# The last expert mixture of a four-layer kernel: the turn of a token tile is issued two beats ahead of its product, and VectorE writes the tiles' row numbers

## What is computed

```python
xn = _layernorm(x, ln_gamma, ln_beta)
xf = xn.reshape(-1, D)                                  # 2048 tokens, D = 128
probs = softmax(clip(xf @ router_w.T))                  # 8 experts
topk_p, topk_i = jax.lax.top_k(probs, 2)
for eid in range(8):
    xe = xf * dense_gate[:, eid:eid + 1]
    gate, up = jnp.split(xe @ gate_up_w[eid].T, 2, axis=-1)   # 256 each
    out = out + (jax.nn.silu(gate) * up) @ down_w[eid].T
return x + out.reshape(B, S, D)                         # and a layer norm behind it
```

## Time and profile before

| | us |
|---|---|
| median of three runs | 1167.92 (1166.6 to 1170.28) |
| the profiled execution, its own time | 1160.82 |
| its span in the trace | 1159.1 |
| from the first turn of the stage (1037.4) to the span's end | 121.7 |

### The profile page before, as it was taken

One profiled execution on the slowest core, in us unless ns is written; L12 is line 12 of the kernel. 1 busy time (PEld: TensorE's weight loads), 2 busy tenths in 40 slices (PEclk: granted clock), 3 DMA queues, 4 the chain that ended last, 5 costly groups with the idle time before them and its releaser, 6 DMA issues.

```text
span 1159.1 us, 18813 instructions
## 1 busy us (share of the span) xinstructions
PE 989.7 (85%) x6456; PEld 501.7 (43%) x6517; DVE 779.2 (67%) x1617; ACT 660.4 (57%) x1282; POOL 364.5 (31%) x587
## 2 busy tenths in 40 slices
PE   5599779999988899276999999798899997988992
PEld 2267534444446588232333333485322232235551
DVE  5976597767743311688888885538888889837665
ACT  4664636565554355243777767573377775765441
POOL 7535511111442245410000002220122122645864
PEclk9799889999999899676999999999799999999996
DMA  5920224333630220233333220003333432311332
GB/s 143 178 60 1 87 86 149 129 125 107 165 89 27 70 64 15 86 107 110 123 102 119 78 73 2 1 1 121 111 123 115 137 85 71 104 40 52 86 90 80
DMA packets 98374, 101.70 MB, mean 88 GB/s; under 512 B 13354, under 2 KB 80571, under 8 KB 98199
## 3 DMA queue, kind: packets, MB, share of 16 engines
q1 hardware_dynamic: 86169, 89.28, 26.4%
q0 software_dynamic: 6432, 8.18, 2.4%
q10 hardware_dynamic: 5680, 3.04, 1.0%
HBM read 66.60 MB, written 38.09 MB: 90 GB/s over the span
## 4 chain that ended last, share of the span: by engine, by line
PE 69%; DVE 16%; ACT 6%; issue 5%; DMA 3%; POOL 2%; SPq 0%; another core or an unknown queue 0%; ACTq 0%; DVEq 0%; POOLq 0%
PE PS L894 13%; PE PS L878 13%; PE PS L851 8%; PE PS L705 6%; PE PS L700 5%; DVE negm L1694 5%; PE PS L1192 4%; PE PS L1063 3%; PE PS L1073 3%; PE PS L881 3%; PE PS L854 2%; PE PS L902 2%; ACT arena L1321 2%; PE PS L1208 2%; ACT arena L1248 2%
## 5 line engine op out<-in xcount | busy, mean ns | idle before, releaser
L1321 ACT ACTIVATE arena<-PS 128x512 f32<-128x512 f32 (+3 forms) x768 | 362.4, 549 | 187.5 <-PE PS L881 118.6
L1694 DVE TENSOR_REDUCE negm<-PS 128x2 f32<-128x1024 f32 (+3 forms) x384 | 404.8, 1088 | 86.4 <-PE PS L851 43.8
L878 PE MATMUL PS<-arena 128*128 128x512 bf16 (+3 forms) x707 | 219.3, 362 | 8.6 <-ACT arena L1321 5.3
L894 PE MATMUL PS<-arena,VPAD 128*32 128x512 f32 (+3 forms) x1536 | 185.9, 555 | 0.1
L851 PE MATMUL PS<-arena 32*128 32x512 bf16 (+3 forms) x768 | 143.2, 373 | 35.0 <-DVE negm L1694 31.0
L851 PEld LDWEIGHTS PS<-arena 32*128 32x128 bf16 x768 | 36.3, 91 | 216.0 <-DVE negm L1694 116.0
L2543 POOL CAST nmp<-negm 128x16 bf16<-128x16 f32 x48 | 9.3, 194 | 357.1 <-DVE negm L1694 240.0
L878 PEld LDWEIGHTS PS<-arena 128*128 128x128 bf16 x768 | 69.7, 98 | 118.0 <-issue 53.9
L700 PE MATMUL PS<-arena,W 128*128 128x512 f32 x144 | 82.0, 703 | 11.0 <-ACT arena L1239 8.5
L705 PEld LDWEIGHTS PS<-W,arena 128*128 128x128 f32 x640 | 80.0, 204 | 15.1 <-issue 7.6
L705 PE MATMUL PS<-W,arena 128*128 128x128 f32 x640 | 81.2, 288 | 3.3 <-DVE arena L1638 2.9
(11 more groups left out here) (335 smaller groups left out, 1542.3 us busy)
## 6 DMA issues: line engine op xcount, KB each, us to landing
arena<-score_q SPq DMA_DIRECT2D x48, 288.0 KB
arena<-score_k SPq DMA_DIRECT2D x48, 288.0 KB
arena<-max_parts SPq DMA_DIRECT2D x48, 256.0 KB
max_parts<-arena SPq DMA_DIRECT2D x36, 256.0 KB, 2.9
score_k<-arena SPq DMA_DIRECT2D x36, 128.0 KB
score_q<-arena SPq DMA_DIRECT2D x12, 384.0 KB
arena<-rows_y SPq DMA_DIRECT2D x16, 256.0 KB, 4.1
arena<-slots SPq DMA_DIRECT2D x46, 65.0 KB, 1.9
```

What stands on the lines that cost most here:

```text
L878: mm = pe.matmul(PS[:, b, q0:S], OK[s][:, r, kt * P:(kt + 1) * P], OQ[s][:, r, q0:S], start=True, stop=True)
L894: mm = pe.matmul(PS[32 * r:32 * r + 32, 7, q0:S], VP[:, u, kt, r, :], PB[:, kt % 2, r, q0:S], start=(kt == 0), stop=True, skip_group_check ...
L1321: act.activation(PB[:, kt % 2, r, q0:S], PS[:, 4 + use % 3, q0:S], ACT.Exp, scale=slope(u % G, r) if o["slope"] else 1.0).then_inc(exped, 1)
L1694: vec.tensor_reduce(negm[:, u % 2, 2 * rp:2 * rp + 2, qt], PS[:, 2 * (use % 2):2 * (use % 2) + 2, 0:nk], AX.X, ALU.max, negate=True).then_ ...
```

## The change

PE's beat b now holds: product of tile b-2, turn of tile b, the expert's number of tile b-1, second product of tile b-4, back transposes of tile b-3. VectorE's beat b: copy of tile b, row number of tile b, h of tile b-2, y of tile b-4. ScalarE's steps stand as before against each other. The turn goes to banks 0 and 2 in turn and waits for the copy of tile t - 2; the back transposes have bank 4 for themselves and wait for the hT copy of the tile before; the second product uses the first 128 columns of bank 7. The table entries move one beat (two on ScalarE, whose count of beats starts at the turn now), which keeps them beside the same product. `expert_at` is multiplied by 768 by VectorE when it is made. `name_of` is gone from POOL, with its place in the order (four tiles ahead, and between the scatters).

```diff
-TAIL_GATES = {5: (2, 2), 6: (2, 6), 7: (2, 6), 8: (2, 6), 9: (2, 3), 10: (2, 8), 11: (2, 5), 12: (2, 6)}
+TAIL_GATES = {6: (2, 2), 7: (2, 6), 8: (2, 6), 9: (2, 6), 10: (2, 3), 11: (2, 8), 12: (2, 5), 13: (2, 6)}
...
-                    if 1 <= beat <= ALL3:
-                        t = beat - 1
+                    if 2 <= beat < ALL3 + 2:
+                        t = beat - 2
                         if t >= 3:
                             pe.wait_ge(hidden3, t - 2)
                         pe.wait_ge(copied3, t + 1)
...
                     if beat < ALL3:
                         t = beat
-                        if t >= 3:
-                            pe.wait_ge(gated3, t - 2)
                         pe.wait_ge(tile_in[t % NTILE], 16 * (t // NTILE + 1))
-                        pe.transpose(PS[:, 2 * (t % 3), 0:P], x3[t % NTILE][:, 0:D], ident).then_inc(turned3, 1)
+                        if t >= 2:
+                            pe.wait_ge(copied3, t - 1)
+                        pe.transpose(PS[:, 2 * (t % 2), 0:P], x3[t % NTILE][:, 0:D], ident).then_inc(turned3, 1)
...
-                    if 2 <= beat < ALL3 + 2:
-                        t = beat - 2
+                    if 3 <= beat < ALL3 + 3:
+                        t = beat - 3
+                        if t >= 1:
+                            pe.wait_ge(gated3, t)
                         pe.wait_ge(hidden3, t + 1)
                         for f in range(2):
-                            mm = pe.transpose(PS[:, 2 * (t % 3), P + f * P:2 * P + f * P], h3[t % 4][:, f * P:(f + 1) * P], ident)
+                            mm = pe.transpose(PS[:, 4, f * P:(f + 1) * P], h3[t % 4][:, f * P:(f + 1) * P], ident)
...
+                        if t >= NBACK:
+                            vec.wait_ge(returned3[i], 16 * (t // NBACK))
+                        vec.wait_ge(tile_in[t % NTILE], 16 * (t // NTILE + 1))
+                        vec.tensor_scalar(name3[:, i:i + 1], x3[t % NTILE][:, D + 1:D + 2], 1.0, float(NOWHERE), ALU.mult, ALU.add).then_inc(named3, 1)
...
-            def name_of(t):
-                i = t % NBACK
-                if t >= NBACK:
-                    pool.wait_ge(returned3[i], 16 * (t // NBACK))
-                pool.wait_ge(tile_in[t % NTILE], 16 * (t // NTILE + 1))
-                pool.tensor_scalar(name3[:, i:i + 1], x3[t % NTILE][:, D + 1:D + 2], 1.0, float(NOWHERE), ALU.mult, ALU.add).then_inc(named3, 1)
```

More of the change, by code:

```diff
@@ L1176, in experts3, with weights_of @@
             def experts3():
-                def expert_of(t):
+                def weights_of(t):
                     if t % TILES == 0:
                         pe.wait_ge(*V.at(WHOLE, f"t{t // TILES}.row"))
-                    return nc.values_load(expert_at[0:1, t:t + 1], engines=[mybir.EngineType.PE], min_val=0, max_val=E - 1,
-                                          skip_runtime_bounds_check_because="the expert is clamped to the last one")
+                    at = nc.values_load(expert_at[0:1, t:t + 1], engines=[mybir.EngineType.PE], min_val=0, max_val=(E - 1) * WIDE3,
+                                        skip_runtime_bounds_check_because="the expert is clamped to the last one")
+                    return WE3[:, bass.ds(at, WIDE3)]
                 pe.wait_ge(ffn3_in, 16 * 2 * E)
                 pe.wait_ge(*ring_freed[-1])
-                experts = {0: expert_of(0)}
-                for beat in range(ALL3 + 3):
-                    if 1 <= beat <= ALL3:
-                        t = beat - 1
+                weights = {}
+                for beat in range(ALL3 + 4):
+                    if 2 <= beat < ALL3 + 2:
+                        t = beat - 2
                         if t >= 3:
@@ L1500, in experts3 @@
             def experts3():
-                for beat in range(ALL3 + 1):
+                for beat in range(ALL3 + 3):
                     if beat in TAIL_SCALAR:
                         last_chunk3(TAIL_SCALAR[beat])
-                    if beat < ALL3:
-                        t = beat
+                    if 2 <= beat < ALL3 + 2:
+                        t = beat - 2
                         if t >= 4:
@@ L2152, in tiles3 @@
                 vec.wait_ge(*V.at(WHOLE, tag + "e"))
[L2153 removed]
+                vec.tensor_scalar(expert_at[:, own], expert[:], float(E - 1), float(WIDE3), ALU.min, ALU.mult).then_inc(*V.did(WHOLE, tag + "expert"))
                 yield
@@ L2202, in experts3 @@
             def experts3():
-                for beat in range(ALL3 + 3):
+                for beat in range(ALL3 + 4):
                     if beat < ALL3:
                         t = beat
+                        i = t % NBACK
                         if t >= 4:
```

60 lines of the change are left out of this document (24 added, 36 removed).

## The result

| | before | after |
|---|---|---|
| median, four runs of each | 1167.26 (1165.4 to 1170.28) | 1151.2 (1148.31 to 1155.35) |
| ratio, with its 95% interval | | 0.9863 (0.9825 to 0.99) |
| the profiled execution, its own time | 1160.82 | 1151.48 |
| its span | 1159.1 | 1149.7 |
| L902 (the last instruction ahead of the stage) to product 14 | 37.57 | 36.42 |

Predicted were 1161.5 and a range of 1157.0 to 1166.5. The direction was right, the time lies 5.8 us under the range. The three lower rows are the stage; together they gave 1.15 + 10.15 + 0.14 = 11.4 us. The spans differ by 9.4 only because the stage began 2.0 us later in the profiled execution of after (L902 at 1037.15 instead of 1035.11), and the change touches nothing ahead of it. One kernel spreads over 5 to 10 us in its runs, so a difference of medians from four runs each is rougher than the stage read in the traces.

What follows compares the result with a forecast made beforehand. A closed loop PE, VectorE, PE, with the copy of the turned tile ending last, was taken to bound the 2.017 us beat. 9.2 - 2.3 - 0.5 = 6.4 us won gave 1161.5, range 1157.0 to 1166.5.

Steps and rivals of the forecast that it cites:

- heavier VectorE beats: Beats where VectorE also carries normalisations or statistics, from product 14 on: predicted to cost 2.3 us in all.
- I take 1.72: Middle of the last expert stage: the beat predicted after the change, from 2.017, winning 9.2 us over 31 beats.
- y loop: Second product, waiting for y of the beat before, behind h and Silu: 3.41 to 3.52 for two beats, 1.70 to 1.76 each.
- hT loop at 1.68: Back transposes, hT copy, weight load, second product, back transposes again: predicted to limit the beat at 1.68 us.
- PE alone at 1.63: PE's own instructions in a beat without a wait: 1.63 us, leaving at most 0.387 of a beat to win.
- The first rival: PE alone sets the beat at 1.63: 10.5 us won, 1157.4; chance 0.12.
- E - 0.73: Delay of a beat by E us of extra VectorE work: 0.37 for a normalisation, 0.47 for statistics.
- A loss of 0.5: Products 0 to 14, where VectorE is the limit: predicted 0.5 us lost, bounds 1 won to 2 lost.
- The name hidden: Row number on VectorE between copy and h: about 0.1 us, hidden in a free beat ahead of h.
- Loads, tail: SP's tile loads have 8.9 us for 1.9, no cost; the 23.9 us behind the last product stay unchanged.
- The name held by GpSimd's DMA: Rival: VectorE's row number waits for a DMA instruction's end, beat 2.12, 6.5 us slower, 1174.4; chance 0.07.
- It has one element a partition: Argument against VectorE's row number being held to a DMA instruction's end, as a 128x4 operation was at 1055.42.

Runs made afterwards that it cites:

- second pair: The same two programs, before and changed, timed again with more runs on the same chip: 1166.04 and 1153.94, ratio 0.9899.
- half product: Changed kernel with a first product of 256 columns instead of 512, waits and orders kept: beats of 1.63 to 1.64 us.
- whole product with a longer lag: Changed kernel with second product and y one beat later, back transposes alternating between banks 4 and 6, all 512 columns kept: ratio 0.9962, beats 1.63 to 1.65.
- names alone: Kernel before with the row numbers moved from GpSimd to VectorE, tiles not turned earlier: 1165.8, ratio 0.9992.
- lead alone: Changed kernel with the row numbers back on GpSimd at their old places: 1156.36, ratio 0.9928.
- the kernel with two columns: Changed kernel with the row number made 128x2 instead of 128x1 on VectorE: ratio 0.9931, beats of 1.63 to 1.65.

## Why the prediction was wrong

The mechanism was right, and nearly each size was on the cautious side. By the steps, with the traces of the first comparison:

| term | predicted | measured |
|---|---|---|
| beat, 31 times | 1.72: +9.2 | 1.64: 31 x 0.377 = +11.7 |
| heavier VectorE beats | -2.3 | -1.5 (52.38 less 31 x 1.64) |
| up to product 14 | -0.5 | +1.15 (+1.87 in the second pair) |
| the end | 0 | +0.1 |
| sum | +6.4 | +11.4 (+12.1) |

- **"I take 1.72" is the step that failed most.** It was the y loop, and in it the term "0.24 back to PE as from the copy" (0.10 of two beats); the loop as it was added up came to 3.41, 1.705 a beat, and 1.72 was taken above that. From y to the second product it is 0.14: y ends at 1101.28 in the rows of the beat, and the weight load starts at 1101.42. A row of before has it too, and the prediction passed it over (timeline of before, VectorE and PE):

```profile
1137.40 0.28 DVE L2222 COPY arena<-PS 128x128 f32<-128x128 f32 x1
1137.82 0.30 PEld L1208 LDWEIGHTS PS<-VPAD,arena 128*128 128x128 f32 x2 [1.07 <-issue]
```

  Why y's hand-over is shorter than those of the copy and of hT isn't shown. That the result of those two is what PE loads as weights doesn't explain it by itself: the output product L990 of after also loads what ScalarE has just copied, and its weight load starts 0.06 after the copy's end.

```profile
1039.81 0.58 ACT L1241 COPY arena<-PS 128x512 f32<-128x512 f32 x1 [2.81 <-PE PS L985]
...
1040.45 1.78 PEld L990 LDWEIGHTS PS<-W,arena 128*128 128x128 f32 x8 [0.86 <-ACT arena L1241]
```

  In after Silu is at +1.12, h +1.70, y +2.10, so the y loop is 2.52 + 0.11 + 0.45 + 0.22 = 3.30 for two beats, 1.65.
- **hT loop at 1.68**: 1.64, measured by the half product. The 0.04 is the second product's 0.48, which is 0.45 when nothing waits.
- **PE alone at 1.63**: 1.64, measured by the whole product with a longer lag. The first rival, with 0.12, was the result for the beat, and the forecast's argument against it, that the y loop is made of rows, was the one that failed; its 1157.4 still was too high, by the first third and by the scatter between executions. The three limits lie within 0.02, where the prediction had spread them over 0.09.
- **Heavy beats.** E - 0.73 gave 0.37 for a normalisation; two beats of after are 2.00 instead of 1.64, 0.36 more (1076.86 to 1078.86 and 1083.77 to 1085.77). But the other two normalisations cost nothing behind product 14, and the 0.8 for the end came to 0.5 (2.14 instead of 1.64 at the statistics). The sum of 1.5 holds another 0.3, the 1.93 between products 36 and 37, which belongs to neither.
- **The first third.** "A loss of 0.5" came from taking the two orders as level, with 1 won as the bound; 1.15 to 1.9 were won. With the names alone product 14 comes 37.56 after L902, no later than before (37.35 and 37.57), so the names cost nothing there, where 0.8 had been put down, and with the lead alone it is 35.69, so the lead wins all of it. It isn't won at the stop: products 7 to 9 take 7.6, and the stop of before, products 6 to 8, 4.05 + 2.28 = 6.3. It is won at the start: product 0 comes 2.0 later after L902 (5.17 for 3.20), as forecast, but products 0 to 2 then take 3.33 for 6.14, and the later beats add 0.3. In the second pair product 0 comes only 1.0 later, where L990 ran at the full clock (1.16 us instead of 2.08), and that is where 1.87 comes from instead of 1.15.
- **The name hidden** (0.1 for it): right, 0.14 long with an end at h's start. **The names' move worth nothing of itself**: right at the old beat only. At 1.64 GpSimd's 1.42 per tile and the layer norm's steps on it would have cost 2.4 us in the last beat, a term that the prediction did not have because it never asked what GpSimd's arrears do without the move.
- **Loads, tail** (23.75 for 23.89): right. **The name held by GpSimd's DMA**: did not occur in 46 of 46. By the Trainium skill (SBUF — State Buffer, Who interferes with whom) a two-port form would have waited for the DMA instruction's end; the 0.14 shows none here. The forecast gave two reasons. "It has one element a partition" held: names of two columns were held where names of one were not. "A name would begin 0.04 behind it" did not: they began anywhere from 0.01 to 0.9 into the instruction. That a held name would hold h was wrong too: in the kernel with two columns h started 0.06 behind the start of a held one.
- **The range.** Its lower end, 1157.0, took the best value for the beat and none of the better values for the other terms. With 12.0 for PE alone, 1 lost to heavy beats and the stated bound of 1 won in the first third it would have reached 1167.92 - 12.0 = 1155.9. The measured 1151.2 is lower still, by the scatter between executions: the second comparison, 1153.94 for 1166.04, lies 12 apart. Of the 10.3 us by which the time missed the forecast, 5.0 are the terms of the sum and the rest is that scatter.

## What to carry to other kernels

When a loop through one engine is opened, work out each remaining loop from rows of the very hand-over that it contains, the same instruction waiting for the same one: in this kernel the prices from an engine's end to PE's weight load are 0.06, 0.14 and 0.24. Limits that come out within a few per cent of each other are one limit; take the one with nothing to mis-size, the engine's own work, and look for it in a beat in which nothing waits. And a helper engine with a little slack at the old beat has none at the new one: what was free to leave there becomes a stop at the first place where someone waits for it.

## What the runs showed of the hardware

- From an engine's end to PE's weight load: 0.14 us from VectorE's y copy to the second product, 0.24 from ScalarE's hT copy to the same product and from VectorE's copy of the turned tile to the first product, 0.06 from ScalarE's copy to the output product L990.
- GpSimd's power takes longer with more elements: 1.04 us for 128x4, 5.46 for 128x32.
- GpSimd's indirect DMA instructions follow each other by 1.28 us (0.97 and 0.30 of issue), by 1.42 with a name of 0.22 between two.
- VectorE's tensor_scalar beside GpSimd's indirect DMA instructions of 0.97 us: 128x1 takes 0.14 wherever it begins; 128x2 takes 0.15 to 0.21 where it begins 0.50 or less into one, and is held to its end where it begins 0.58 to 0.74 into it (five of five); a 128x4 that began 0.54 in was held too (0.46).
- PE's drawn busy time says little on its reserve: 40.47 of 42 us at a beat of 2.00, 41.71 at 1.64.
- The same program took 1166 on one chip and 1185 on four others, 1.6% more; half or more of it is one stop of 11 to 15 us in this stage. Whether it is the chip, and what makes the stop, stays open.
- PE's granted clock fell behind idle stretches of 2.1 us in some traces and not in others (0.52 and 1.00 over the same beat), and behind the longer ones of the stop to 0.50; one to three beats later it stood at 1.00 again. A beat of 1.64 takes 3.20 at 0.50.
- A table load on ScalarE takes 1.28 us, and the one exp between two Silus has two of them.
